# The last six expert additions alternate over the second and third sum, and the first sum is loaded early, gated and added to x by itself

## What is computed

```python
h = _layernorm(x, axis=-1) * (1 + ca) + sa
x = x + ga * _L0_attn_ref(h, ...)          # 16 heads of 16, rotary, causal
h = _layernorm(x, axis=-1) * (1 + cb) + sb
x = x + gb * _L0_ffn_ref(h, ...)           # the part that the change touches
```

```python
ye = jnp.einsum('eci,eih->ech', h, down_proj)
y_flat = jnp.where(valid[:, None], ye[flat_e, jnp.minimum(pos, C - 1)], 0.0)
y = jnp.sum(y_flat.reshape(-1, K, H) * topw.reshape(-1, K)[..., None], axis=1)
```

## Time and profile before

| what | value |
|---|---|
| runs, us | 294.72, 296.07, 296.50 (median 296.07) |
| the profiled execution, us | 295.17 |
| its span from first to last instruction, us | 293.4 |
| granted TensorE clock, mean | 0.979 |
| busy share of the span: PE, DVE, ACT, POOL | 90%, 73%, 54%, 54% |
| expert loop and its additions | 170 to 261 us |
| own products, last additions, loads, fold and stores | 261 to 293.4 us |

### The profile page before, as it was taken

How to read it: one execution, slowest core, us unless ns; L and a number is a source line. 1 busy time by engine, 2 the same in 40 slices (tenths; PEclk the granted TensorE clock), 3 DMA queues, 4 the chain that set the end, 5 groups by cost and what they waited for, 6 DMA issues and landing times.

```text
span 293.4 us, 6906 instructions
## 1 busy us (share of the span) xinstructions
PE 265.2 (90%) x2077; PEld 198.0 (68%) x2077; DVE 214.2 (73%) x658; ACT 157.4 (54%) x466; POOL 158.6 (54%) x156
## 2 busy tenths in 40 slices
PE   7899999998999899789777889999999999999980
PEld 2355677556756567556432568888888888889980
DVE  4497776888778967882442357899999898995386
ACT  4478498337853487354622456666666666631000
POOL 3651000004556545677777775878877888887000
PEclk9999999999999999999995999999999999999996
DMA  6999699999999524997595659999988999666943
GB/s 244 333 342 332 157 345 363 366 263 267 317 320 285 163 76 152 313 342 226 162 296 174 179 158 224 241 199 165 162 152 157 157 159 168 76 67 79 308 154 113
DMA packets 62123, 64.23 MB, mean 219 GB/s; under 512 B 5069, under 2 KB 57618, under 8 KB 62096
## 3 DMA queue, kind: packets, MB, share of 16 engines
q1 hardware_dynamic: 51664, 49.06, 58.2%
q0 software_dynamic: 10272, 14.85, 26.0%
q10 hardware_dynamic: 160, 0.01, 0.0%
HBM read 35.93 MB, written 28.45 MB: 219 GB/s over the span
## 4 chain that ended last, share of the span: by engine, by line
PE 52%; DVE 13%; POOL 10%; issue 8%; DMA 7%; ACT 6%; SPq 1%; DVEq 0%; ACTq 0%; POOLq 0%
PE bank L1290 13%; PE bank L1304 8%; POOL slot_rows L629 5%; POOL slot_rows L638 5%; PE bank L957 4%; PE bank L1281 4%; PE bank L969 2%; DMA arena<-sum 2%; PE bank L1033 2%; PE bank L1031 2%; PE bank L1298 2%; PE bank L1017 2%; PE bank L1063 2%; PE bank L988 2%; ACT arena L712 2%
## 5 line engine op out<-in xcount | busy, mean ns | idle before, releaser
L629 POOL DMA_INDIRECT slot_rows<-stage x48 | 48.1, 1002 | 29.1 <-issue 7.0
L1290 PE MATMUL bank<-arena,stage 128*128 (+1 forms) x256 | 53.1, 329 | 0.0
L663 POOL DMA_INDIRECT sum<-kz,stage x24 | 37.5, 1564 | 10.8 <-issue 5.4
L1290 PEld LDWEIGHTS bank<-arena,stage 128*128 128x128 f32 x256 | 40.3, 190 | 1.0 <-issue 0.4
L1304 PE MATMUL bank<-arena,stage 96*128 (+1 forms) x128 | 39.0, 387 | 0.0
L886 ACT ACTIVATE stage<-bank 128x256 f32<-128x256 f32 x64 | 24.5, 383 | 22.6 <-PE bank L1281 22.6
L1454 DVE TENSOR_REDUCE rmax<-bank 128x2 f32<-128x512 f32 (+1 forms) x48 | 30.6, 683 | 4.7 <-PE bank L988 4.4
L663 POOL DMA_INDIRECT sum<-stage x16 | 25.5, 1596 | 5.5 <-issue 3.4
L1281 PE MATMUL bank<-cst,stage 128*128 128x128 f32 x128 | 25.1, 276 | 2.8 <-DMA stage<-slot_rows 2.5
L893 ACT ACTIVATE stage<-bank 128x96 f32<-128x96 f32 x64 | 16.0, 251 | 18.8 <-PE bank L1290 17.9
L618 POOL COPY stage<-slot_idx 128x16 uint32<-128x16 uint32 x2 | 0.4, 196 | 47.3 <-DVE slot_idx L1553 47.3
(11 more groups left out here) (214 smaller groups left out, 637.4 us busy)
## 6 DMA issues: line engine op xcount, KB each, us to landing
slot_rows<-zero_row SPq DMA_DIRECT2D x8, 1040.0 KB, 12.3
stage<-slot_rows SPq DMA_DIRECT2D x64, 130.0 KB, 3.4
arena<-in_gate_up SPq DMA_DIRECT2D x10, 768.0 KB, 12.3
arena<-in_down SPq DMA_DIRECT2D x5, 768.0 KB, 13.7
sum<-zero_row SPq DMA_DIRECT2D x3, 1152.0 KB, 12.2
arena<-sum SPq DMA_DIRECT2D x12, 256.0 KB, 5.5
arena<-in_gate_up SPq DMA_DIRECT2D x2, 864.0 KB, 6.9
arena<-in_wmod SPq DMA_DIRECT2D x1, 1024.0 KB, 6.7
```

Source lines behind the costliest of these rows:

```text
L629: pool.indirect_dma_start(slot_rows, bass.IndirectOffsetOnAxis(ap=idx[:, t, k:k + 1], axis=0), src[:, t, :], None, bounds_check=last_slot, ...
L663: pool.indirect_dma_start(sums[a], where, ye_ring[i % RING], None, compute_op=ALU.add).then_inc(added[a], 16)
L1290: last = mm(bank[2 + q % 2][:, 0:GU + 1], xeT[:, q % 2, k * CAP:(k + 1) * CAP], expert_w[:, s - 1, k * (GU + 1):(k + 1) * (GU + 1)], start ...
```

## The change

The last six additions (i = 46 to 51) no longer take the three sums in turn but only sums 1 and 2 in alternation. Sum 0 is complete with addition 45. The numbers of additions are now 16, 18 and 18. `fold_order` becomes sum 0, sum 1 (last addition 50), sum 2 (last addition 51).

SyncE loads the parts of sum 0 for b = 0 and 1 when addition 45 has landed, for b = 2 when addition 46 has, and for b = 3 when addition 47 has. The loads of sum 1 and sum 2 wait for additions 50 and 51.

VectorE gates each part of sum 0 and adds it to x by itself. The own bank and the part of the third sum are now folded into the part of sum 1, which is gated and added to x after that.

```diff
+    LAST_TWO = 6
 def sum_of(i):
-    return i % NACC
+    return i % NACC if i < NADD - LAST_TWO else 1 + (i - NADD + LAST_TWO) % 2
...
 for a in fold_order:
     sp.wait_ge(added[a], 16 * adds_before(NADD, a))
     for b in range(B):
+        if a == whole and b >= 2:
+            i = NADD - LAST_TWO + b - 2
+            sp.wait_ge(added[sum_of(i)], 16 * adds_before(i + 1, sum_of(i)))
         sp.dma_start(part[:, a, b, :, :], ...)
...
+a0, a1, a2 = fold_order
-def add_sum(b, a):
-    dve.wait_ge(sum_ld[a][b], 16)
-    return V.tensor_tensor(part[:, whole, b, :, :], part[:, whole, b, :, :], part[:, a, b, :, :], ALU.add)
+def add_sum(b):
+    dve.wait_ge(sum_ld[a1][b], 16)
+    dve.wait_ge(sum_ld[a2][b], 16)
+    return V.tensor_tensor(part[:, a1, b, :, :], part[:, a1, b, :, :], part[:, a2, b, :, :], ALU.add)
 def add_late(b):
+    dve.wait_ge(sum_ld[a1][b], 16)
     dve.wait_ge(p_late, b + 1)
     (part[:, whole, b] becomes part[:, a1, b])
-def gated(b):
-    s0 = part[:, whole, b, :, :]
+def gated(b, a):
+    dve.wait_ge(sum_ld[a][b], 16)
+    rows_in = part[:, a, b, :, :]
     (two instructions as before, on rows_in)
...
-dve.wait_ge(sum_ld[a0][0], 16)
+for b in range(B):
+    link(gated(b, a0))
 link(add_late(0))
-dve.wait_ge(sum_ld[a0][1], 16)
 link(add_late(1))
-for b in (0, 1, 3, 2):
-    dve.wait_ge(sum_ld[a0][b], 16)
-    link(add_sum(b, a1))
-link(gated(B - 1))
+link(gated(B - 1, a1))
 for b in range(B - 1):
     if b == 2:
         link(add_late(b))
-    link(add_sum(b, a2))
-    gated(b).then_inc(v_out, 1)
+    link(add_sum(b))
+    gated(b, a1).then_inc(v_out, 1)
 gated_late(B - 1).then_inc(v_out, 1)
```

More of the change, by code:

```diff
@@ L1733, in _ @@
                 pick_tokens(n, 0, TOK)
-            def add_sum(b, a):
-                dve.wait_ge(sum_ld[a][b], 16)
-                return V.tensor_tensor(part[:, whole, b, :, :], part[:, whole, b, :, :], part[:, a, b, :, :], ALU.add)
+            a0, a1, a2 = fold_order
[3 more added lines that the diff above has]
+                return V.tensor_tensor(part[:, a1, b, :, :], part[:, a1, b, :, :], part[:, a2, b, :, :], ALU.add)
             def add_late(b):
+                dve.wait_ge(sum_ld[a1][b], 16)
                 dve.wait_ge(p_late, b + 1)
-                return V.tensor_tensor(part[:, whole, b, :, :], part[:, whole, b, :, :],
+                return V.tensor_tensor(part[:, a1, b, :, :], part[:, a1, b, :, :],
                                        bank[b][:, :].rearrange("p (t h) -> p t h", t=TPB), ALU.add)
@@ L1747, in out_rows @@
                 return x_sb[:, TPB * b:TPB * b + TPB, :]
-            def gated(b):
-                s0 = part[:, whole, b, :, :]
-                link(V.tensor_tensor(s0, s0, gbB[:, b:b + 1, :].broadcast_to([P, TPB, H]), ALU.mult))
-                return V.tensor_tensor(out_rows(b), out_rows(b), s0, ALU.add)
+            def gated(b, a):
+                dve.wait_ge(sum_ld[a][b], 16)
+                rows_in = part[:, a, b, :, :]
+                link(V.tensor_tensor(rows_in, rows_in, gbB[:, b:b + 1, :].broadcast_to([P, TPB, H]), ALU.mult))
+                return V.tensor_tensor(out_rows(b), out_rows(b), rows_in, ALU.add)
             def gated_late(b):
@@ L1760, in gated_late @@
                 return V.tensor_tensor(out_rows(b), out_rows(b), late_t[:, :, :], ALU.add)
-            a0, a1, a2 = fold_order
-            dve.wait_ge(sum_ld[a0][0], 16)
+            for b in range(B):
+                link(gated(b, a0))
             link(add_late(0))
-            dve.wait_ge(sum_ld[a0][1], 16)
             link(add_late(1))
-            for b in (0, 1, 3, 2):
-                dve.wait_ge(sum_ld[a0][b], 16)
-                link(add_sum(b, a1))
-            link(gated(B - 1))
+            link(gated(B - 1, a1))
             for b in range(B - 1):
```

## The result

The changed kernel takes 297.60 us (median of 22 runs, 295.44 to 300.05), the kernel before 296.36 in 22 runs beside it. The ratio is 1.0047, with a 95% interval of 1.0024 to 1.0070: 0.2 to 0.7% slower. The forecast was 293.2 us, 0.8% faster, with a range of 291.3 to 295.8. So the sign was wrong, and the size of the effect is small.

What follows compares the result with a forecast made beforehand. The bound was the chain from GpSimd's additions over SyncE's loads to VectorE. Two fewer instructions (1.44 us) and an earlier landing (0.9) gave 2.4 us off the four-run mean of 295.6: 293.2 us, range 291.3 to 295.8.

Steps and rivals of the forecast that it cites:

- the term for 47: GpSimd's addition 47, with two early loads right on it, takes 4.85 us to land, between 3.7 and 5.7.
- The terms for 48 and 49: GpSimd's additions 48 and 49, one early load beside each, take 4.4 and 4.5 us to land.
- For the fourth I take 3.9: SyncE's fourth load of sum 1 (b = 3) takes 3.9 us and lands at 278.4, between 276.6 and 280.5.
- The price of the alternation: GpSimd's last six additions: waiting two places back makes a pair need 4.56 us instead of 3.70, 0.43 us an addition.
- The early loads' landing was hidden: Sum 0's last load lands at 272.1, while VectorE, using them from 268.05, works on b = 2 of that sum.
- the eight gates: VectorE's eight new gate and add instructions, 5.8 us, fit its idle time from 268.05 to 273.9 and cost nothing.
- two instructions fewer: VectorE has 12 instructions instead of 14 before the last gate, after sum 1's b = 3 part lands: 1.44 us less.
- the place named for addition 51: A VectorE pause after its gate of b = 3 would show the prediction wrong, with addition 51 deciding.
- rival 1: TensorE becomes the bound as additions are hardly slowed; end no earlier than 286.9, time 291.7 to 292.3; chance 28%.
- Rival 3: Slower: additions 47, 49 and 51 chain with slow landings; addition 51 landing at 279.1 or later, example 296.6; chance 8%.
- Rival 2: VectorE's gates and GpSimd's last additions disturb each other; addition 51 lands 1.4 us later, time 294.4; 16% together with rival 4.
- The test given for a wrong prediction: One of three signs: sum 1's part for b = 3 lands at 279 or later, against the forecast 278.4.

Runs made afterwards that it cites:

- e10: The changed kernel itself run once more, for a second profile; ratio 1.0019 to the kernel before.
- e9: The changed kernel with all four loads of sum 0 issued at once when addition 45 has landed; ratio 1.0043 to the kernel before.
- e3: The kernel before with the last six additions alternating over two sums, its own fold, and sum 0 loaded only when addition 49 has landed; ratio 1.0039.
- e1: The changed kernel with the four loads of sum 0 issued only when addition 49 has landed; ratio 1.0025 to the kernel before.
- e4: The kernel before with two spare 256 KB loads issued when addition 45 has landed, sums still in turn; ratio 1.0002.
- e5: The changed kernel with only VectorE's new fold kept: sums in turn and loads as in the kernel before; ratio 0.9987.
- e8: The kernel before with TensorE also adding the second sum's part for the last sequence, and VectorE's gate of that sequence moved ahead; ratio 0.9952, 294.62 us.
- e2: The changed kernel with VectorE waiting for addition 49 to land before gating sum 0; ratio 1.0016 to the kernel before.
- e6: The changed kernel with sum 0 loaded one part at a time, after additions 45, 46, 47 and 48; ratio 1.0012 to the kernel before.

## Why the prediction was wrong

Counted from the start of addition 46:

| us | before | forecast | changed | again (e10) |
|---|---|---|---|---|
| 47, start to landing | 3.7 | 4.85 | 6.6 | 6.1 |
| 48, the same | 4.2 | 4.4 | 4.7 | 4.6 |
| 49 starts | 6.2 | 7.5 | 9.8 | 9.3 |
| 51 starts | 9.9 | 12.7 | 14.7 | 14.2 |
| part a1, b = 3, issue to landing | 6.0 | 3.9 | 5.5 | 4.7 |
| the same part lands | 20.1 | 19.2 | 23.1 | 21.6 |
| from there to VectorE's end | 11.5 | 10.0 | 10.0 | 10.7 |
| D | 31.6 | 29.2 | 33.1 | 32.3 |

The 5.1 us for 48 in the expectations was read from the wait for it, which GpSimd passed at 271.20. The last of the addition's 16 semaphore updates stands in the trace at 270.79. GpSimd passed that wait 1.18 us after the one for 47, and so it did in e9 and e10: a wait that follows another closely tells only the latest time of a landing.

**The step that failed** is the term for 47 in "With the early loads beside them I take 4.85 us for 47 ..., 4.4 and 4.5 for 48 and 49". The mechanism was in the text, the size was not: 47 took 6.6 and 6.1 us and lay outside the bound of 5.7, which was the nearest row of the expert loop. There the DMA was fuller (206 GB/s), but no load of 256 KB was issued beside the addition. The terms for 48 and 49 held roughly (4.7 and 4.6, 4.1 and 4.1). The right row was the one of addition 51, 6.85 us behind loads, and for 47 I didn't use it. The wait of 49 added 0.7 us that nothing foretold, so 49 started 2.3 us later than forecast, and 50, the trigger of the a1 loads, 2.0.

**The second miss** is "For the fourth I take 3.9": it took 5.5 and 4.7. Fewer loads ahead of it did not make it as fast as I had counted on. Addition 51 moves its packets at that time, but no run tests whether that is the reason. The 4.4 us that the prediction worked out from the Trainium skill (DMA: Bandwidth & Descriptors, Anatomy of one DMA) is nearer, and below both. The page gives its figure for DMAs that GpSimd issues, and these are SyncE's. Together with the first miss and 0.3 us for the landing of 50 this is the whole difference of 3.9 us in the landing of the part.

**The price of the alternation** was worked out as 1.2 us for addition 51 without loads; e3 and e1 measured 1.7 and 2.5, of which about 0.7 is the longer start of 49 behind its wait. e3 shows it in the time too. All seven timed comparisons of kernels with the alternation over six additions came out above the kernel before (1.0012 to 1.0047), the three that keep the turn or nearly keep it, with the loads or the fold changed, at 1.0002, 0.9987 and 0.9982. They are not independent: e1 to e4, e5 to e8, and e9 with e10 each share their runs of the kernel before. Taking back the early loads (e1) or the early gates (e2) did not bring the time measurably below the changed kernel's. For e1 the trace says why: the early loads cost the additions some 2 us (51 starts at 14.7 and 14.2 with them, at 12.4 without), but without them VectorE's 17.2 us start late. They pay for about what they cost.

**What was right.** The early loads' landing was hidden, the eight gates cost VectorE no time on the path (beside them 49, ahead of 50, took 1.93 and 1.81 us on GpSimd instead of 1.55), two instructions fewer stood behind the decisive load (10.0 us instead of 11.5), and VectorE ran without a pause from there on in the first profile. In the second it paused 0.69 us ahead of the part a2, b = 0, the place named for addition 51. The TensorE bound of rival 1 was never reached in the changed kernel.

**The rivals.** Rival 3 named the mechanism, the chain of two with slow landings. Its point of decision was the landing of 51 at 279.1 or three landings of 16.5 us; they came to 15.3 and 15.6. The kernel was slower below that point. In the first profile the a1 loads, which hang on addition 50, decided. In the second, VectorE did wait for the part a2, b = 0. It landed at 282.9 on the clock of before (the start of 46 set to 259.18), later than the 282.3 that rival 3 names, though 51 itself had landed early enough. So rival 3 had the cause and, in part, the wrong place. It was given 8%, too little, because I counted how long the loads stand beside an addition (1.4 us) and not that the addition can come behind all of them. Rival 2 is theory V: 0.2 to 0.4 us for each of two or three additions, not a whole VectorE instruction. The test given for a wrong prediction, part a1, b = 3 landing at 279 or later, was met: 282.3 on the clock of before.

A ratio of +0.2 to +0.7% and a D that rose by 1.5 and 0.7 us fit in size, but a single D has some 1 us of scatter, so the parts are shown in the traces and their sum in the time only roughly.

## What to carry to other kernels

A transfer that is moved into an idle-looking stretch is not free when a chain of small dependent transfers runs there. Ask which of them it is issued just ahead of, and how much slack that one has in its chain; shortening a rotation of buffers takes exactly that slack away. Count the work behind the last landing first: giving one part of it to TensorE, whose work ended 3.9 us before it was needed (e8), won 0.5% without touching any transfer.

## What the runs showed of the hardware

Loads of 256 KB that are issued just after the start of an indirect addition make it land later, by 0.7 to 1 us each (the row of numbers under e9). In the changed kernel, with two loads issued 0.16 and 0.55 us after its start, no packet of 47 moved until more than 3 us after that start, while the engines were only 76% busy in the 1.5 us from 1.57 us on. In e6, with one load, the packets of both moved side by side. So it isn't shown that an addition always waits for a whole load. Loads issued 1.4 to 1.5 us after the start seem to count too: such additions landed after 4.5 us (51 in the changed kernel), 5.4 (51 in e10) and 5.7 (50 in e3).

Addition 49 started 1.39 us after its wait had ended in all seven profiles with the alternation over six additions, with picks or gates on VectorE, with early loads and without. Others that waited for a landing started after 0.71 us (48 and 51 in the changed kernel). What the other 0.68 us are was not settled.

GpSimd's share of an indirect addition took 1.75 to 1.93 us beside VectorE's gates (two SBUF inputs, 128 x 512 values) in seven of ten cases, and 1.55 in all seven with VectorE idle (51 before and in the first profile of the changed kernel, among others). The Trainium skill (SBUF — State Buffer, SBUF: two separate sides) has a lock between a VectorE instruction with two SBUF inputs and a GpSimd instruction that reads SBUF, held for the whole instruction. The traces bear this out only in part: three of the ten additions were not longer, and the added 0.2 to 0.4 us are less than one VectorE instruction of 0.69. Nor is it the gates alone. Beside VectorE's picks, additions took up to 2.06 us in the kernel before (48) and 2.24 in e9 (48), and 51 in e8 took 1.88 with only the last 0.47 us of a pick beside it.
